# Reordering the openings of the three stages of a stencil, attention and expert kernel

## The reference

```
f     = x * A, x * B grids;  df = -grad(A f) + 0.5 * grad2(B f)         # layer 0: stencil, 5 grids of 512 x 512
x     = max(f + dt * df, 0)
x     = ln(x) * (1 + scale[t]) + shift[t]                               # scale, shift = silu(sin_emb(t)) @ W_ada + b_ada
q,k,v = x@Wq+bq, x@Wk+bk, x@Wv+bv                                       # 16 heads of 32
p     = softmax(q k^T / sqrt(32) + bias, masked)                        # bias: 8 x 16 x 512 x 512
x     = x + (p v) @ Wo + bo                                             # layer 1, attention
x     = x + gelu2((ln(x)*g2+beta2) @ W1 + b1) @ W2 + b2                 # layer 1, plain feed-forward, 512 -> 2048 -> 512
x     = ln(x + gelu(x @ Wi[e] + bi[e]) @ Wo[e] + bo[e]) * gamma[e] + beta[e]   # layer 2, one expert per batch
x     = x + gate(mean(x)) * (x @ basis @ basis^T[:, :32] @ resp_w^T + biases)  # layer 3, basis by Gram-Schmidt
```

## Time and profile before

| | us |
|---|---|
| median of 3 runs | 2770.02 (2769.93 to 2770.68) |
| the profiled run | 2768.22 |
| its span | 2766.3 |
| PE busy | 2639.3 (95%) |
| DVE busy | 1697.8 (61%) |
| ACT busy | 1024.1 (37%) |
| POOL busy | 1025.2 (37%) |
| start of attention in the span | 205.5 |
| start of the plain layer in the span | 1195.9 |

### The profile page before, as it was taken

One profiled execution on the slowest core, in us unless ns is written; L12 is line 12 of the kernel. 1 busy time (PEld: TensorE's weight loads), 2 busy tenths in 40 slices (PEclk: granted clock), 3 DMA queues, 4 the chain that ended last, 5 costly groups with the idle time before them and its releaser, 6 DMA issues. The chain is left out here.

```text
span 2766.3 us, 46266 instructions
## 1 busy us (share of the span) xinstructions
PE 2639.3 (95%) x17072; PEld 2037.0 (74%) x17088; DVE 1697.8 (61%) x3341; ACT 1024.1 (37%) x2160; POOL 1025.2 (37%) x756
## 2 busy tenths in 40 slices
PE   7975999999999999969999999999999999999997
PEld 2434777777777777657888888888787887888775
DVE  9976777777777777756444444445554564565443
ACT  1114666666666666611111111111223232322222
POOL 1005677776777777533100110012222322322210
PEclk9997999999999999989999999999999999999998
DMA  4234564655646555531111011103333343244311
GB/s 173 107 132 128 164 194 139 188 154 180 189 144 188 145 185 164 153 105 54 31 31 31 1 31 31 31 1 124 115 103 106 111 134 125 89 130 126 104 46 38
DMA packets 212972, 305.99 MB, mean 111 GB/s; under 512 B 14604, under 2 KB 93516, under 8 KB 210064
## 3 DMA queue, kind: packets, MB, share of 16 engines
q1 hardware_dynamic: 211662, 301.99, 35.3%
q0 software_dynamic: 1088, 1.05, 0.2%
HBM read 268.94 MB, written 34.04 MB: 110 GB/s over the span
## 5 line engine op out<-in xcount | busy, mean ns | idle before, releaser
L815 POOL TENSOR_TENSOR at_bias<-at_bias,at_mask 128x1024 f32<-128x1024 f32 x224 | 483.0, 2160 | 247.3 <-DMA at_bias<-in_fside_Bx16xSxS 245.9
L1180 DVE CUSTOM_DVE_ANT_0 at_bias<-at_bias,at_bank_score 128x512 f32<-128x512 f32 x512 | 338.4, 682 | 186.9 <-PE at_bank_score L1046 140.3
L96 PE MATMUL ff_bank_out<-ff_WH,ff_gH 128*128 128x512 f32 x1024 | 407.9, 398 | 1.9 <-DVE ff_gL L1939 1.9
L96 PE MATMUL ff_bank_hid<-ff_hH,ff_WH 128*128 128x512 f32 x1024 | 402.2, 393 | 2.8 <-DVE ff_WL L1892 2.8
L1667 ACT ACTIVATE ff_g<-ff_bank_hid,ff_b1c 128x512 f32<-128x512 f32 x256 | 175.5, 686 | 607.7 <-PE ff_bank_hid L98 607.7
L98 PE MATMUL ff_bank_out<-ff_WH,ff_gL 128*128 128x512 f32 x1024 | 400.3, 391 | 0.0
L97 PE MATMUL ff_bank_out<-ff_WL,ff_gH 128*128 128x512 f32 x1024 | 399.9, 391 | 0.0
L97 PE MATMUL ff_bank_hid<-ff_hL,ff_WH 128*128 128x512 f32 x1024 | 399.8, 390 | 0.0
L98 PE MATMUL ff_bank_hid<-ff_hH,ff_WL 128*128 128x512 f32 x1024 | 399.7, 390 | 0.0
L1939 DVE TENSOR_TENSOR ff_gL<-ff_g,ff_gH 128x512 fp32r<-128x512 f32 x256 | 178.7, 698 | 348.9 <-ACT ff_g L1667 344.4
L1566 POOL TENSOR_SCALAR ff_WH<-shared 128x1024 fp32r<-128x1024 f32 x144 | 177.1, 1230 | 568.9 <-PE ff_bank_out L98 330.5
(11 more groups left out here) (310 smaller groups left out, 4282.2 us busy)
## 6 DMA issues: line engine op xcount, KB each, us to landing
at_bias<-in_fside_Bx16xSxS SPq DMA_DIRECT2D x256, 512.0 KB, 3.8
shared<-in_L_cond_Wi SPq DMA_DIRECT2D x128, 256.0 KB, 2.9
shared<-in_L_cond_Wo SPq DMA_DIRECT2D x128, 256.0 KB, 3.0
shared<-x_after_layer SPq DMA_DIRECT2D x64, 256.0 KB, 5.2
st_f<-in_x SPq DMA_DIRECT2D x8, 1024.0 KB, 6.9
x_after_attention<-shared SPq DMA_DIRECT2D x32, 256.0 KB, 2.3
shared<-x_after_attention SPq DMA_DIRECT2D x32, 256.0 KB, 4.4
shared<-in_L_cond_W SPq DMA_DIRECT2D x32, 256.0 KB, 3.0
```

Source lines behind the costliest of these rows:

```text
L96: pe.matmul(out, wh, xh, start=first, stop=False)
L815: pool.tensor_tensor(bias[i % NB][:, :, :], bias[i % NB][:, :, :], mask[:, i // 2 % R, :].unsqueeze(1).to_broadcast([P, 2, S]), ALU.add).t ...
L1180: dve.tensor_tensor_reduce(t, t, pS[u % HC][:, :], -1.0, 3.0e38, ALU.add, ALU.min, nmax[:, u % 4:u % 4 + 1]).then_inc(s_max, 1)
```

## The change

Only orders are changed, and no arithmetic is.

- **Stencil.** B2 and f[0] are loaded in halves of two rows, in turn (four transfers of 512 KB). DVE makes the first G in halves as they come, then the border columns, V in halves, cQp, Qp; the angles stand behind Qp, cQm and the three steps that end emb behind them, then Qm. PE starts V's products with the first half. POOL sets the border weights first, then the matrices, and issues its nine transfers last.
- **Attention, first batch.** The four transposes get four banks. DVE's `weights_low(0)` moves behind the shifts, `weights_low(2)` ahead of q's low half, `weights_high(2)` on ACT ahead of q's; number 3 moves into the loop (ACT at unit 9, DVE at unit 11). POOL makes one half of the mask, waits for all four low halves of x, adds the mask to three biases, then makes the other half; the output bias moves to units 8 to 14.
- **Plain layer.** DVE takes the statistics of the plain layer's first batch in the last attention batch, at units 40 to 44, and POOL the inverse root at unit 49. SP no longer waits for the last stores at the end of attention; the load of batch 1 in the plain layer waits for them. POOL issues g2 and beta2 first and does the memsets behind the high halves of two weight units.

```diff
@@ stencil, sync @@
-            sp.dma_start(B2[:, :, :], rows_of(grids["B2"])).then_inc(b2_in, 16)
-            sp.dma_start(f[0][:, :, :], rows_of(a["x"][0])).then_inc(s_f[0], 16)
+            for k, half in enumerate(first_halves):
+                sp.dma_start(B2[:, half, :], rows_of(grids["B2"])[:, half, :]).then_inc(s_bhalf[k], 16)
+                sp.dma_start(f[0][:, half, :], rows_of(a["x"][0])[:, half, :]).then_inc(s_fhalf[k], 16)
@@ stencil, tensor @@
+                if n == 0:
+                    pe.wait_ge(s_vhalf, 1)
+                    for r, m, k in ((0, quarter, 1), (3, vup, 0), (1, nquarter, 0), (2, nquarter, 1)):
+                        pe.matmul(out[:, r, :], m, v[:, k, :], start=True, stop=False)
+                    pe.wait_ge(s_prod, 1)
+                    for r, m, k in ((1, quarter, 2), (2, quarter, 3), (3, nquarter, 2), (0, nvdown, 3)):
+                        pe.matmul(out[:, r, :], m, v[:, k, :], start=False, stop=False)
@@ stencil, vector @@
+            def first_g_product():
+                for k, rows in enumerate(first_halves):
+                    dve.wait_ge(s_bhalf[k], 16)
+                    dve.wait_ge(s_fhalf[k], 16)
+                    t_ = dve.tensor_tensor(G[:, rows, 1:D + 1], B2[:, rows, :], f[0][:, rows, :], ALU.mult)
+                t_.then_inc(s_g, 1)
...
+                if n == 0:
+                    for rows, made in zip(first_halves, (s_vhalf, s_prod)):
+                        dve.tensor_tensor(V[0][:, rows, :], G[:, rows, 2:W], G[:, rows, 0:D], ALU.subtract).then_inc(made, 1)
+                    return
...
                     dve.tensor_tensor(cQp[:, :, :], B0[:, :, :], A0[:, :, :], ALU.subtract).then_inc(s_coef, 1)
+                    dve.wait_ge(s_coef, 1)
+                dve.tensor_tensor(Qp[slot][:, :, :], cQp[:, :, :], fs, ALU.mult).then_inc(s_prod, 1)
+                if n == 0:
+                    angles()
                     dve.tensor_tensor(cQm[:, :, :], B0[:, :, :], A0[:, :, :], ALU.add).then_inc(s_coef, 1)
+                    silu()
                     dve.wait_ge(s_coef, 2)
-                dve.tensor_tensor(Qp[slot][:, :, :], cQp[:, :, :], fs, ALU.mult).then_inc(s_prod, 1)
                 dve.tensor_tensor(Qm[slot][:, :, :], cQm[:, :, :], fs, ALU.mult).then_inc(s_prod, 1)
@@ attention @@
+        first_x = (pS[0], pJ[1], pT[0], pT[1])
...
-            for r in range(R):
-                sp.wait_ge(s_st[r], 16 * B)
...
-            for half in range(2):
-                make_mask(0, half)
+            make_mask(0, 0)
+            pool.wait_ge(s_xl, C)
             for i in range(3):
                 if i not in ON_PE:
                     add_mask(0, i)
-            pool.wait_ge(s_const, 64)
-            for r in range(R):
-                out_bias(0, 0, r)
+            make_mask(0, 1)
...
+                    if n == B - 1 and u == 49:
+                        pool.wait_ge(s_next_var, 1)
+                        pool.tensor_tensor(next_rstd[:, :], next_var[:, :], mhalf[:, :], ALU.pow)
...
+                    if is_first(n) and u in (8, 10, 12, 14):
+                        out_bias(0, 0, (u - 8) // 2)
@@ attention, scalar @@
             act.wait_ge(s_const, 64)
+            weights_high(2)
             act.wait_ge(s_bq, 1)
             q_high(0, 0)
             k_high(0, 0)
-            weights_high(2)
             copy_v(0, 0)
             exp(0, 0)
-            weights_high(3)
...
+                    if is_first(n) and u == 9:
+                        weights_high(3)
@@ attention, vector @@
             mean_var(0)
-            weights_low(0)
             dve.wait_ge(s_ab, 32)
...
+            weights_low(0)
             for m in range(C):
                 x_low(0, 0, m)
             weights_low(1)
+            weights_low(2)
             dve.wait_ge(s_bq, 1)
             q_low(0, 0)
             k_low(0, 0)
-            weights_low(2)
             copy_vT(0, 0)
             sum_scores(0, 0)
             sum_scores(0, 1)
-            weights_low(3)
...
+                    if is_first(n) and u == 11:
+                        weights_low(3)
...
+                    if n == B - 1 and 40 <= u < 40 + R:
+                        next_row_stats(u - 40)
+                    if n == B - 1 and u == 44:
+                        next_mean_var()
@@ feed_forwards, sync @@
             def load_row(n, r):
+                if n == 1:
+                    sp.wait_ge(s_before[r], 16 * B)
@@ feed_forwards, gpsimd @@
-            power(1)
-            for g in range(highs_by(-1)):
+            first_highs = highs_by(-1)
+            high(0)
+            high(1)
+            pool.memset(ones[:, :], 1.0).then_inc(s_cm, 1)
...
+            for g in range(2, first_highs):
                 high(g)
@@ feed_forwards, vector @@
-            ln_stats(0)
+            dve.wait_ge(s_first, 16 * R)
             ln_apply(0)
```

140 lines of the change are left out of this document (81 added, 59 removed).

## The result

The changed kernel takes **2751.64 us** (median of four runs: 2750.12, 2750.95, 2752.34, 2756.08), beside 2769.97 us for the kernel before in the same series: ratio 0.9936, 95% interval 0.9924 to 0.9948, that is 18 us (14 to 21) less. The forecast was 2753.0 us, range 2746 to 2760. The profiled execution took 2750.12 us, span 2748.2 us, so again about 2 us lie outside the span.

The account below looks back on a forecast made before the run. PE was taken as the bound, so time counts only where PE stands still, chiefly in three openings. Stencil +1.0, attention opening -10.0, plain opening with stage change -8.4, statistics +0.4 make -17.0: 2770.02 to 2753.0 us, range 2746 to 2760.

Parts of the forecast that it names:

- Stencil, +1.0: Stencil: VectorE waits for f's second half and A0, so the second V comes 1.0 us later, bounds 0.3 to 2.
- the cover: Stencil: VectorE's 1.64 us wait for PE's scale and shift products, taken to absorb part of its 2.6 us delay.
- Scale and shift beside the mask adds, -6.3: Attention opening: with mask adds held back, eight scale and shift steps shorten, so the shifts end 6.3 us earlier.
- the stretch behind S: Attention opening: work after the shifts' end (225.35 us before), where Wq's low half moves, delaying x's low halves about 0.3 us.
- Clock in the opening: Attention opening: PE at granted clock 0.51 for v's product, which takes 5.3 us as before.
- Wv's load and its low half: Attention opening: load issued at 221.45, landing 5.5 to 7 us later; low half done at 230.7 to 232.9.
- Up to the ninth exp -2.1, Wo in the loop +2.4: Attention's first units: taking Wo out of the opening gains 2.1 us; its steps inside the loop cost 2.4.
- Stage change, -1.7, and statistics, +0.4: Attention's end: no wait for last stores, plain layer starts 1.7 us earlier; statistics in the last batch cost 0.4.
- Plain opening, -6.7 behind the start: Plain layer opening: early statistics let first evacuation start 6.7 us after stage start, limited by constants; 6.7 us gained there.
- The batches unchanged: Loops behind the openings: attention batches stay about 117 us apart, so 0 us change.
- Port and chain: Rival: pieces moved into the loop and beside masks paid in full, stencil loses 2; 2758.5 us, to 2762; chance 0.20.
- All hidden: Rival: PE keeps the higher clock through q, k, v and Wo costs nothing; 2748 us, to 2745; chance 0.12.

Follow-up runs that it names:

- e5: Kernel after with VectorE's low half of Wq put back ahead of the shifts: 2748.47 us, ratio 0.9918.
- e6: Kernel after with both halves of Wo back in attention's opening: 2753.88 us, ratio 0.9936.
- e8: Kernel after with the plain layer's four first constants in their own buffers, loaded in the last attention batch: 2751.98 us, ratio 0.9934.
- e10: Kernel of e8 with GpSimd's memsets and selection at the plain layer's front, U and V issues behind the second high half: 2750.22 us.
- e11: Kernel after with old stencil, Wq's low half in VectorE's gap, mask adds held until Wv's low half, e10's plain opening: 2742.90 us, ratio 0.9903.

## Why the prediction was right, point by point

- **Stencil, +1.0.** The chain (f's second half, A0, the vanished wait) is in the trace of after and gives 1.1. The small steps ahead ended at 7.1 us, not 8.3, so that VectorE also waited for the first half (0.95 us). f's second half landed at 11.9 instead of 10.5, since its issue had moved from 2.66 to 3.61 us. A0, issued at 4.87 instead of 3.62, landed 1.0 us later than forecast too; it was waited for less (0.80 instead of 1.35) only because VectorE came later. The mis-sized term is the cover: 1.64 us was one trace's; on average the part costs 0.3.
- **Scale and shift beside the mask adds, -6.3.** Right: 0.7 apiece. The shifts end 8.1 us earlier behind the stage's start, of which 1.9 are the next point's.
- **The first inverse root.** Not in the sum. The forecast moved Wq's low half for its effect on Wv's load and on the stretch behind S, and read the root's 2.98 us as its length. It was a wait for that same low half (e5), worth 1.9 us. This is the step that failed: the exclusive port, which the text weighed against the change, also speaks for it at this place. The Trainium skill, "SBUF — State Buffer", section "SBUF: two separate sides", says that whichever of the two operations starts first gets the shared port pair for the whole instruction, and the other blocks. The trace agrees: 2.99 us where VectorE's step began 0.2 us earlier, 1.04 without it.
- **Clock in the opening.** The forecast had PE at 0.51 for v's product in full. It was at 1.00 for k and still for the first 0.7 us behind the pause of 3.85 us, then at 0.50 until 236.9 us, still within the product, so that this took 4.6 us instead of 5.3. Together with the root and some quicker evacuations this makes the first exp 12.9 us earlier behind the stage's start, where the forecast had 10.2.
- **Wv's load and its low half.** Landed 5.3 us behind its issue (forecast 5.5 to 7); the low half finished at 232.0, 25.3 us behind the stage's start (forecast 25.2 to 27.4). Right, port included.
- **Up to the ninth exp -2.1, Wo in the loop +2.4.** Measured in e6 against five traces: -2.7 and +1.7. Right within the clock's spread.
- **Stage change, -1.7, and statistics, +0.4.** -1.8 and, within the traces' spread, +0.2.
- **Plain opening, -6.7 behind the start.** Measured -4.0. Two terms were too small. The last constant was issued 0.4 us later than forecast and landed 5.0 us behind its issue instead of 3.4, so ScalarE started 2.0 us late; the weights' loads had left 1.8 to 3.7 us before this issue, 2.4 to 4.3 before the same one in before, and whether they made the difference isn't tested. Then, from the first evacuation to the first hidden product, 3.5 us passed instead of 2.5: VectorE's first cast and split, beside GpSimd's memsets and selection, took 0.87 and 1.62 us instead of 0.42 and 0.69. For this price of the port 0.3 us stood in the sum. So 2.0 us are the constants and 0.7 the port, which are the missing 2.7.
- **The batches unchanged.** The inverse roots in attention's loop are 116.6 to 117.5 us apart (before: 116.3 to 117.1); the plain and the expert batches lost 0.1 us each, by the buffers' place.
- **Rivals.** "Port and chain" had its mechanism in both openings, for 1.8 us at Wv's low half and more at the splits. "All hidden" had a part of its clock in after's trace: v's product took 4.6 us, between the 5.3 of before and the 2.8 that the forecast gives for the full clock. Neither took over, and the errors cancelled: on average -13.2 instead of -10 in attention, -5.7 instead of -8.0 around the plain layer, 0.3 instead of 1.0, and 1.2 for the buffers, which no term had. The total was right to 1.4 us, the terms were off by up to 3.2: that part is luck.

## What to carry to other kernels

A short step of GpSimd that looks too long (2.98 us for 128 x 4) is a wait in disguise: look what VectorE runs beside it, and who is served first. Around an opening, the gain of an earlier first product shrinks as long as later steps are stretched and PE pauses at the low clock: e8 brought the product 4.0 us forward and gained 1.7 up to the first loop root, and e10 and e11, which took away the stretched splits, 1.5 to 2.3 more. And a term of a few us in an opening wants more than one trace of the same code, which unrelated experiments give for nothing, and a look at the granted clock of both traces before a difference is put down to the change.
